# Softmax rows of an attention layer split into fp16 halves and transposed by DMA instead of TensorE

## The chip, the cores and the metric

The kernel runs on one core of a Trainium2 chip. The number is device time in microseconds for one launch. Before the change it is 2286.52 us, the median of three runs (2285.9 to 2289.88). All times of single instructions are from one profiled execution.

## What is computed

The input x is 128 examples of 128 tokens by 384 channels, and adj holds one 128x128 matrix per example. Two layers follow each other, both with a residual. Layer A is attention with 12 heads of 32 channels and a full bias of 2·adj; layer B has three causal "experts" of 128 channels, mixed by a gate.

```python
# layer A (x here is the layernormed input)
q = (x @ Wq.T), k = (x @ Wk.T), v = (x @ Wv.T + bv)      # 12 heads of 32
scores = einsum('bqhd,bkhd->bhqk', q, k) * scale + 2 * adj[:, None]
p = softmax(scores)                                      # rows that are all zero give 0
out = einsum('bhqk,bkhd->bqhd', p, v) @ Wo.T + bo
# layer B (x here is the layernormed sum)
q, k = x @ Wqk + bqk; expert 0's q goes through a 3-tap convolution over tokens
expert 1 takes 4 global keys more (masked by the causal mask, as columns past 128)
y_e = causal_softmax(q_e k_e^T / sqrt(128)) @ (x @ Wv[e] + bv[e])
out = (y * gate_weights) @ Wp + bp                       # top 2 of 3 experts
```

## The kernel before

The 128 examples are worked in 32 groups of four. Matmuls on projections are done in three fp16 passes (hi·hi, hi·lo, lo·hi), where each fp32 operand has been split into a rounded fp16 part and an fp16 remainder. ScalarE writes the rounded part (called hi), VectorE the remainder (lo). Scores, softmax and the mix p·v of layer A work in fp32, the scores on stacked fp16 parts in one matmul.

Nothing is scheduled at run time. Five tables of words give the order of the steps on TensorE (`pe`), ScalarE (`act`), VectorE (`dve`), GpSimd (`pool`) and the SyncE queue (`sp`). Each engine goes through its list strictly in order and waits on semaphores. `FIRST_STEPS` and `LAST_STEPS` are the ramps; `ORDER_OF_STEPS` is one turn, repeated 30 times. A word such as `A.mix.2` is step mix of layer A for example 2 of the group; `A.score.2.1` is the second third (four heads) of example 2. In one turn the engines work on three groups: the layer-A steps that `ahead` names (hT, qk, stack) on the newest, the rest of layer A on the one before it, layer B on the one before that.

The steps of layer A for one example b, with the lines of the profile:

- *hT*: GpSimd writes the normed rows (L1082), ScalarE (L699) and VectorE (L948) split them, and SyncE issues a DMA that transposes both fp16 parts through the crossbar (L495, tile h1T). *qk*, *v*: projections (L534). *stack*: 24 SBUF-to-SBUF DMAs in each group lay the parts of q and k out for the scores (L509, tiles Qs and Ks); the first score of a group waits for all 24.
- *score*: four heads a step on TensorE (L603); VectorE adds the bias, takes the row minimum of the negated score and writes raw_score (L978). *smax* (L984) reads raw_score once more for the maximum. ScalarE takes the exponential out of raw_score into S[b % 2] with the row sum (L738). *norm*: VectorE makes the row factor, GpSimd multiplies S by it in three pieces (L1125).
- *turn*: TensorE transposes S, four heads a step (L616), and ScalarE moves the result from PSUM to PT (L752). *mix*: 12 fp32 matmuls with 32 columns of v (L628), which land in four column strips of the array. *proj*: VectorE adds the residual xres (L1021), which GpSimd has made of xin and bo_row (L1111). *ln2* prepares layer B.

PSUM has a ring of five banks for A and three for B; a step on TensorE waits until the step five (three) places before it on its layer's list has been evacuated.

## Time and profile before

| | |
|---|---|
| runs | 2286.52 us (2285.9 to 2289.88) |
| profiled execution | 2291.18 us, of which the span from first to last instruction is 2289.4 us |
| busy share of the span | PE 95%, DVE 81%, ACT 65%, POOL 51% |
| granted TensorE clock | 0.991 of full speed |
| DMA engines | 29.9% of the 16 engines' span in the main queue |

PE is TensorE's matmul unit, DVE is VectorE, ACT is ScalarE, POOL is GpSimd, SP the SyncE queue. A row's "busy" is the time covered by its instructions; since instructions of one engine overlap at their ends, the distance from start to start is the cost of a step in a row of steps, and the mean duration is somewhat more than that. A DMA has two times: what its issue takes on the SP queue, and the time until it has landed.

### The profile page before, as it was taken

How to read it: one execution, taken by the hardware profiler on the slowest of the kernel's cores; microseconds unless marked ns; L12 is line 12 of the kernel's file. 1: busy time of each engine (PE TensorE's matmuls, PEld its weight loads, DVE VectorE, ACT ScalarE, POOL GpSimd, SP SyncE). 2: the span in 40 equal slices, each digit the busy share in tenths (PEclk: the TensorE clock that was granted, in tenths of full speed). 3: DMA queues.
4: the chain of work that ended last, by engine and by line, in shares of the span. 5: the costliest groups of instructions: out<-in, count | busy, mean ns of one | idle time of the engine just before them, and what ended most of it. 6: DMA issues, size and time to landing. Idle time of an engine off the chain costs nothing.

```text
span 2289.4 us, 51173 instructions
## 1 busy us (share of the span) xinstructions
PE 2172.9 (95%) x16557; PEld 1385.8 (61%) x16557; DVE 1855.0 (81%) x7182; ACT 1492.9 (65%) x5330; POOL 1159.8 (51%) x1553
## 2 busy tenths in 40 slices
PE   4699999999999999999999999999999999999998
PEld 2366666666666666666656666656666656666655
DVE  5788887888888788887778887888887888877884
ACT  2676666676666676666666665766666766666763
POOL 2645554455554455554445554455555455554452
PEclk9899999999999999999999999999999999999999
DMA  6312334322333322323313333223333223333210
GB/s 186 70 38 70 88 75 89 73 48 71 89 75 89 72 48 72 88 75 88 72 43 77 84 79 88 60 50 83 78 85 89 59 50 83 79 85 89 44 32 28
DMA packets 244665, 168.36 MB, mean 74 GB/s; under 512 B 119216, under 2 KB 243760, under 8 KB 244400
## 3 DMA queue, kind: packets, MB, share of 16 engines
q1 hardware_dynamic: 242208, 163.80, 29.9%
q8 instruction: 134, 2.20, 0.4%
q10 hardware_dynamic: 2192, 1.29, 0.2%
q14 instruction: 131, 1.07, 0.2%
HBM read 39.18 MB, written 25.17 MB: 28 GB/s over the span
## 4 chain that ended last, share of the span: by engine, by line
PE 78%; DVE 9%; DMA 5%; ACT 3%; SPq 2%; issue 2%; POOL 1%; POOLq 0%; DVEq 0%
PE A_bank L534 30%; PE B_bank L534 24%; PE A_bank L616 6%; DMA h1T<-h_parts 4%; PE B_bank L610 4%; PE A_bank L628 4%; PE B_bank L635 4%; PE A_bank L603 3%; DVE smax L984 3%; DVE h_parts L948 2%; PE B_bank L620 2%; PE B_bank L580 2%; DVE raw_score L978 2%; ACT h_parts L699 1%; POOL h L1082 1%
## 5 line engine op out<-in xcount | busy, mean ns | idle before, releaser
L738 ACT ACTIVATE S<-raw_score,smin 128x128 f32<-128x128 f32 x1536 | 594.9, 393 | 94.6 <-DVE smin L978 94.6
L1125 POOL TENSOR_TENSOR S<-S,rowf 128x512 f32<-128x512 f32 x384 | 415.7, 1110 | 398.3 <-DVE rowf L1003 398.3
L978 DVE CUSTOM_DVE_ANT_0 raw_score<-A_bank,adj,s_unit 128x128 f32<-128x128 f32 x1536 | 433.5, 345 | 18.6 <-PE A_bank L603 15.9
L1130 POOL TENSOR_TENSOR S<-S,row2f 128x384 f32<-128x384 f32 x128 | 105.8, 826 | 499.6 <-DVE row2f L1011 496.8
L738 ACT ACTIVATION_READ_ACCUMULATOR S<-raw_score,smin 128x1 f32 x1536 | 294.7, 192 | 0.0
L534 PE MATMUL A_bank<-h1T,wq_hi 128*128 128x512 f16 x576 | 177.0, 390 | 76.4 <-DMA h1T<-h_parts 76.3
L616 PE MATMUL A_bank<-ident,S 128*128 128x128 f32 x1536 | 218.2, 275 | 5.5 <-POOL S L1125 5.5
L984 DVE TENSOR_REDUCE smax<-raw_score 128x12 f32<-128x1536 f32 x128 | 223.0, 1743 | 0.0
L752 ACT ACTIVATE PT<-A_bank 128x512 f32<-128x512 f32 x384 | 210.3, 591 | 6.7 <-PE A_bank L616 6.0
L534 PE MATMUL A_bank<-wv_hi,h1T 128*128 128x384 f16 x768 | 199.3, 328 | 5.9 <-DVE wv_lo L771 5.0
L616 PEld LDWEIGHTS A_bank<-ident,S 128*128 128x128 f32 x1536 | 178.2, 142 | 31.6 <-issue 11.7
L703 ACT ACTIVATE b_hT_hi<-B_bank 128x512 f16<-128x512 f32 x96 | 53.2, 587 | 190.4 <-PE B_bank L580 190.4
L534 PE MATMUL A_bank<-h1T,wk_hi 128*128 128x512 f16 x576 | 171.3, 379 | 0.7 <-DVE smin L978 0.7
L752 ACT ACTIVATE PT<-B_bank 128x384 f32<-128x384 f32 x128 | 62.8, 491 | 160.0 <-PE B_bank L620 159.8
L1082 POOL TENSOR_SCALAR h<-xin,stat 128x384 f32<-128x384 f32 x128 | 89.2, 699 | 129.0 <-DVE h_parts L948 128.7
L745 ACT ACTIVATE S<-S,s2min 128x128 f32<-128x128 f32 x384 | 149.0, 395 | 3.8 <-DVE s2min L988 3.8
L603 PE MATMUL A_bank<-Ks,Qs 96*128 96x128 f16 x1536 | 133.8, 219 | 3.5 <-DMA Ks<-k_hi 2.3
L534 PEld LDWEIGHTS A_bank<-h1T,wq_hi 128*128 128x128 f16 x576 | 53.7, 99 | 136.9 <-issue 74.3
L988 DVE CUSTOM_DVE_ANT_0 S<-B_bank,later 128x128 f32<-128x128 f32 x384 | 90.9, 286 | 55.6 <-PE B_bank L610 55.3
L603 PEld LDWEIGHTS A_bank<-Ks,Qs 96*128 96x128 f16 x1536 | 110.6, 98 | 36.3 <-issue 3.2
L534 PE MATMUL B_bank<-wv2g_hi,b_hT_hi 128*128 128x416 f16 x384 | 130.2, 339 | 0.0
L534 PE MATMUL B_bank<-wv2g_hi,b_hT_lo 128*128 128x416 f16 x384 | 130.1, 339 | 0.0
(183 smaller groups left out, 5975.6 us busy)
## 6 DMA issues: line engine op xcount, KB each, us to landing
xin<-in_x SPq DMA_DIRECT2D x32, 768.0 KB, 4.9
Qs<-q_hi SPq DMA_DIRECT2D x256, 96.0 KB, 2.2
out<-x1res SPq DMA_DIRECT2D x128, 192.0 KB, 2.1
Ks<-k_hi SPq DMA_DIRECT2D x252, 96.0 KB, 3.2
Qs<-q_lo SPq DMA_DIRECT2D x128, 96.0 KB, 2.2
Ks<-k_lo SPq DMA_DIRECT2D x126, 96.0 KB, 2.9
adj<-in_adj SPq DMA_DIRECT2D x32, 256.0 KB, 5.7
h1T<-h_parts SPq DMA_TRANSPOSE x128, 2.9
```

The costliest lines, as they stand in the source:

```text
L534: mm = nc.tensor.matmul(dst, left(c)[a], right(c)[b], start=(c == 0 and n == 0), stop=(c == KC - 1 and n == 2))
L603: mm = nc.tensor.matmul(dst[:, tok(j)], Qs[:, c * HPC + j, tok(b)], Ks[:, c * HPC + j, tok(b)], start=True, stop=True)
L610: mm = nc.tensor.matmul(dst[:, tok(e)], q2[:, e, tok(b)], k2[:, e, tok(b)], start=True, stop=True)
L616: mm = nc.tensor.transpose(dst[:, tok(j)], S[b % 2][:, c * HPC + j, :], ident[:])
L738: ins = nc.scalar.activation(S[b % 2][:, h, :], raw_score[:, h, :], ACT.Exp, bias=smin[b % 2][:, h:h + 1], scale=-1.0, accum_out=ssum[b % ...
L745: ins = nc.scalar.activation(S2[b % 2][:, e, :], S2[b % 2][:, e, :], ACT.Exp, bias=s2min[b % 2][:, e:e + 1], scale=-1.0, accum_out=s2sum[b ...
L752: nc.scalar.activation(dst, src[:, 0:dst.shape[1]], ACT.Copy).then_inc(evacuated[stage, "act"], 1)
L978: ins = nc.vector.tensor_tensor_reduce(raw_score[:, h, :], src[:, j * T:(j + 1) * T], adj2[:, b, :], s_unit[:], 3.0e38, ALU.add, ALU.min, ...
L984: nc.vector.tensor_reduce(smax[b % 2][:], raw_score[:], AXX, ALU.max).then_inc(maxed, 1)
L1082: nc.gpsimd.tensor_scalar(h1[:, b % 2, :], xin[g % 2][:, b, :], stat[g % 2][:, 0, b:b + 1], stat[g % 2][:, 1, b:b + 1], ALU.add, ALU.mult) ...
L1125: nc.gpsimd.tensor_tensor(S[b % 2][:, hs, :], S[b % 2][:, hs, :], rowf[b % 2][:, hs].unsqueeze(2).broadcast_to([P, HPC, T]), ALU.mult).the ...
L1130: nc.gpsimd.tensor_tensor(S2[b % 2][:], S2[b % 2][:], row2f[b % 2][:].unsqueeze(2).broadcast_to([P, NE, T]), ALU.mult).then_inc(normed2, 1)
```

## The change

The softmax rows of layer A no longer go through TensorE to be transposed. After the row factor has been applied (it now holds 2^14 more, so that fp16 has range), ScalarE rounds each third of S to fp16 and GpSimd subtracts to get the remainder. SyncE issues one crossbar transpose per third, with both parts, into PT. The values v are split in the same way: VectorE writes V, ScalarE the fp16 part, GpSimd the remainder (step vl). The mix takes 36 fp16 matmuls in place of 12 fp32 ones and the factor 2^-14 is taken out when its result is split.

Besides: the exponential is taken in place, with S[b % 2] in the place of raw_score, so it now waits for smax (`maxed`); the scores of example b wait until the remainder of example b-2 has been taken (`p_lo`). The residual is added into xin in place, so the load of x for the group after next waits for the group's last proj and goes to the end of the SP list. h1_parts is a ring of two. The row guard in norm is a chain of four small instructions, as before. The first gate step is one instruction shorter. Scores of layer B wait for the turn of two examples before. All order tables are new.

```diff
+P_SCALE = 2.0 ** 14
 def ahead(step):
-    return step[0] == "A" and step[1] in ("hT", "qk", "stack", "h1")
+    return step[0] == "A" and step[1] in ("ln1", "h1", "hT", "qk", "stack")
...
-        xres = sb("xres", [P, GB, C])
-        h1_parts = sb("h1_parts", [P, GB, 2, C], F16)
+        h1_parts = sb("h1_parts", [P, 2, 2, C], F16)
-        V = sb("V", [P, GB, C])
+        V = sb("V", [P, 2, C])
+        V_parts = sb("V_parts", [P, GB, 2, C], F16)
-        raw_score = sb("raw_score", [P, NH, T])
-        PT = [sb(f"PT{k}", [P, HPC * T]) for k in range(KC)]
+        P_parts = sb("P_parts", [P, KC, 2, HPC * T], F16)
+        PT = [sb(f"PT{k}", [P, KC, 2 * HPC, T], F16) for k in range(2)]
@@ SyncE @@
-                if (stage, kind) == ("A", "res") and g + 2 < NG:
-                    sp.wait_ge(xres_ready, count(g, GB, GB))
-                    sp.wait_ge(h1_ready, count(g, GB, GB))
+                if (stage, kind) == ("A", "load") and g + 2 < NG:
+                    wait_evacuated(sp, ("A", "proj", GB - 1, 0), g)
                     sp.dma_start(xin[g % 2][:], dram_group(x, g + 2)).then_inc(x_loaded[g % 2], 16)
+                if (stage, kind) == ("A", "turn"):
+                    sp.wait_ge(p_lo, count(g, GB * KC, b * KC + third + 1))
+                    if third == 0 and b >= 2:
+                        wait_products(sp, ("A", "mix", b - 2, 0), g)
+                    elif third == 0 and not g == 0:
+                        wait_products(sp, ("A", "mix", b + 2, 0), before(g))
+                    sp.dma_start_transpose(PT[b % 2][:, third, :, :],
+                                           P_parts[:, third, :, :].rearrange("p n k -> p (n k)"))\
+                        .then_inc(p_turned[third], 16)
@@ TensorE @@
-                elif kind == "turn" and A:
-                    pe.wait_ge(normed, count(g, GB * KC, b * KC + c + 1))
-                    for j in range(HPC):
-                        mm = nc.tensor.transpose(dst[:, tok(j)], S[b % 2][:, c * HPC + j, :], ident[:])
                 elif kind == "mix" and A:
-                    wait_evacuated(pe, ("A", "v", b, 0), g)
+                    pe.wait_ge(v_lo, count(g, GB, b + 1))
                     for k in range(KC):
-                        wait_evacuated(pe, ("A", "turn", b, k), g)
-                        for j in range(HPC):
-                            h = k * HPC + j
-                            mm = nc.tensor.matmul(dst[j * HD:(j + 1) * HD, tok(k)], V[:, b, h * HD:(h + 1) * HD],
-                                                  PT[k][:, tok(j)],
-                                                  start=True, stop=True)
+                        pe.wait_ge(p_turned[k], count(g, 16 * GB, 16 * (b + 1)))
+                        for n, (v_part, p_part) in enumerate([(0, 0), (1, 0), (0, 1)]):
+                            for j in range(HPC):
+                                h = k * HPC + j
+                                mm = nc.tensor.matmul(dst[j * HD:(j + 1) * HD, tok(k)],
+                                                      V_parts[:, b, v_part, h * HD:(h + 1) * HD],
+                                                      PT[b % 2][:, k, p_part * HPC + j, :],
+                                                      start=(n == 0), stop=(n == 2))
@@ ScalarE @@
+                if kind == "v":
+                    wait_evacuated(act, step, g)
+                    if not g == 0:
+                        wait_products(act, ("A", "mix", b, 0), before(g))
+                    nc.scalar.activation(V_parts[:, b, 0, :], V[:, b % 2, :], ACT.Copy).then_inc(v_hi, 1)
+                elif kind == "turn" and A:
+                    act.wait_ge(normed, count(g, GB * KC, b * KC + c + 1))
+                    if not (g == 0 and b == 0):
+                        act.wait_ge(p_turned[c], count(g, 16 * GB, 16 * b))
+                    nc.scalar.activation(P_parts[:, c, 0, :],
+                                         S[b % 2][:, c * HPC:(c + 1) * HPC, :].rearrange("p j k -> p (j k)"),
+                                         ACT.Copy).then_inc(p_hi, 1)
                 elif kind == "score" and A:
                     wait_evacuated(act, step, g)
+                    act.wait_ge(maxed, count(g, GB, b + 1))
-                        ins = nc.scalar.activation(S[b % 2][:, h, :], raw_score[:, h, :], ACT.Exp,
+                        ins = nc.scalar.activation(S[b % 2][:, h, :], S[b % 2][:, h, :], ACT.Exp,
@@ VectorE @@
                 elif kind == "score" and A:
-                    if not (g == 0 and b == 0):
-                        dve.wait_ge(exped, count(g, GB * KC, (b - 1) * KC + c + 1))
-                        dve.wait_ge(maxed, count(g, GB, b))
+                    if b >= 2 or not g == 0:
+                        dve.wait_ge(p_lo, count(g, GB * KC, (b - 2) * KC + c + 1))
                 elif kind == "score":
+                    if b >= 2:
+                        wait_products(dve, ("B", "turn", b - 2, 0), g)
+                    elif not g == 0:
+                        wait_products(dve, ("B", "turn", b + 2, 0), before(g))
@@ GpSimd @@
+                elif kind == "vl":
+                    pool.wait_ge(v_hi, count(g, GB, b + 1))
+                    nc.gpsimd.tensor_tensor(V_parts[:, b, 1, :], V[:, b % 2, :], V_parts[:, b, 0, :],
+                                            ALU.subtract).then_inc(v_lo, 1)
+                elif kind == "turn":
+                    pool.wait_ge(p_hi, count(g, GB * KC, b * KC + c + 1))
+                    nc.gpsimd.tensor_tensor(P_parts[:, c, 1, :],
+                                            S[b % 2][:, c * HPC:(c + 1) * HPC, :].rearrange("p j k -> p (j k)"),
+                                            P_parts[:, c, 0, :],
+                                            ALU.subtract).then_inc(p_lo, 1)
-                    nc.gpsimd.tensor_tensor(xres[:, b, :], xin[g % 2][:, b, :], bo_row[:], ALU.add).then_inc(xres_ready, 1)
+                    pool.wait_ge(h1_ready, count(g, GB, b + 1))
+                    nc.gpsimd.tensor_tensor(xin[g % 2][:, b, :], xin[g % 2][:, b, :], bo_row[:],
+                                            ALU.add).then_inc(xres_ready, 1)
```

One row of the new table, as a specimen (SyncE's turn; the row of before is `A.hT.0 A.hT.1 A.hT.2 A.hT.3 A.stack.0 A.res A.adj A.stack.1 B.proj.0 ...`):

```diff
+        A.hT.0 A.turn.0.0 A.hT.1 A.turn.0.1 A.turn.0.2 A.hT.2 A.hT.3 A.turn.1.0 A.turn.1.1 A.turn.1.2 A.adj
+        A.turn.2.0 A.turn.2.1 A.turn.2.2 A.stack.0 A.turn.3.0 A.turn.3.1 A.turn.3.2 A.stack.1 B.proj.0 B.proj.1
+        B.proj.2 B.proj.3 A.load
```

The order on three engines, in the middle of a steady turn. First SyncE's queue over one turn, before, with its DMAs in the order of their issue:

```order
L495 DMA_TRANSPOSE h1T<-h_parts 128x6x128 x4
L509 DMA Qs<-q_hi 32x3x512 x8
L509 DMA Qs<-q_lo 32x3x512 x4
L488 DMA xin<-in_x 128x4x384
L514 DMA adj<-in_adj 128x4x128
L509 DMA Ks<-k_hi 32x3x512 x4
L509 DMA Ks<-k_lo 32x3x512 x4
L509 DMA Ks<-k_hi 32x3x512 x4
L517 DMA out<-x1res 128x384 x4
```

And now, from the last two transposes of h1T on (ahead of them stand two of h1T and the three of example 0, taking turns):

```order
L501 DMA_TRANSPOSE h1T<-h_parts 128x6x128 x2
L510 DMA_TRANSPOSE PT<-P_parts 128x8x128 x3
L530 DMA adj<-in_adj 128x4x128
L510 DMA_TRANSPOSE PT<-P_parts 128x8x128 x3
L525 DMA Qs<-q_hi 32x3x512 x8
L525 DMA Qs<-q_lo 32x3x512 x4
L510 DMA_TRANSPOSE PT<-P_parts 128x8x128 x3
L525 DMA Ks<-k_hi 32x3x512 x4
L525 DMA Ks<-k_lo 32x3x512 x4
L525 DMA Ks<-k_hi 32x3x512 x4
L533 DMA out<-x1res 128x384 x4
L494 DMA xin<-in_x 128x4x384
```

Twelve transposes of eight blocks each have come in, three of them between the stacking of q and that of k, and the load of x has moved to the end.

Then GpSimd from the norm of example 1 to that of example 3, before (S<-S,rowf is the norm of layer A, S<-S,row2f that of layer B, h<-xin the normed rows of the next group):

```order
L1125 TENSOR_TENSOR S<-S,rowf 128x512 x3
L1082 TENSOR_SCALAR h<-xin,stat 128x384 x4
L1125 TENSOR_TENSOR S<-S,rowf 128x512 x3
L1130 TENSOR_TENSOR S<-S,row2f 128x384 x2
L1120 TENSOR_TENSOR x1res<-x,bp_row 128x384
L1125 TENSOR_TENSOR S<-S,rowf 128x512 x3
```

And the same stretch now (P_parts<-S,P_parts is the remainder of a third of the softmax rows, V_parts<-V,V_parts that of v):

```order
L1167 TENSOR_TENSOR S<-S,rowf 128x512 x3
L1137 TENSOR_TENSOR V_parts<-V,V_parts 128x384
L1141 TENSOR_TENSOR P_parts<-S,P_parts 128x512 x3
L1167 TENSOR_TENSOR S<-S,rowf 128x512 x3
L1141 TENSOR_TENSOR P_parts<-S,P_parts 128x512 x2
L1162 TENSOR_TENSOR x1res<-x,bp_row 128x384
L1141 TENSOR_TENSOR P_parts<-S,P_parts 128x512
L1152 TENSOR_TENSOR xin<-xin,bo_row 128x384
L1137 TENSOR_TENSOR V_parts<-V,V_parts 128x384
L1152 TENSOR_TENSOR xin<-xin,bo_row 128x384
L1167 TENSOR_TENSOR S<-S,rowf 128x512 x3
```

Between two norms there are now three subtractions of 128x512 that were not there, and the normed rows of the next group have moved ahead of this piece.

Last, TensorE around the mix of example 0, before:

```order
L534 MATMUL B_bank<-b_hT_hi,wk_lo 128x512
L628 MATMUL A_bank<-PT,V 32x128 x12
L616 MATMUL A_bank<-ident,S 128x128 x8
L534 MATMUL B_bank<-b_hT_hi,wk_hi 128x512
L534 MATMUL B_bank<-b_hT_lo,wk_hi 128x512
```

And now:

```order
L618 MATMUL A_bank<-Ks,Qs 128x128 x8
L639 MATMUL A_bank<-PT,V_parts 32x128 x36
L618 MATMUL A_bank<-Ks,Qs 128x128 x4
L550 MATMUL A_bank<-h1T,wq_hi 128x512 x2
L550 MATMUL A_bank<-h1T,wq_lo 128x512
```

The transposes are gone, a mix has 36 short matmuls, and the first mix stands between the scores of example 3, where before it came ahead of them.

## Rows read from the trace of the kernel before

**Rows 1.** The page's busy times: engine, busy us, share, instructions.

```profile
PE 2172.9 (95%) x16557; PEld 1385.8 (61%) x16557; DVE 1855.0 (81%) x7182; ACT 1492.9 (65%) x5330; POOL 1159.8 (51%) x1553
```

**Rows 2.** The page's chain that ended last, by engine.

```profile
PE 78%; DVE 9%; DMA 5%; ACT 3%; SPq 2%; issue 2%; POOL 1%; POOLq 0%; DVEq 0%
```

**Rows 3.** Timeline of the SP queue: start, duration, instruction; a turn's first transposes.

```profile
139.89 6.46 SPq L495 DMA_TRANSPOSE h1T<-h_parts  x4
...
2138.67 6.47 SPq L495 DMA_TRANSPOSE h1T<-h_parts  x4
```

**Rows 4.** Windows, one turn: length, busy per engine, clock, DMA share, GB/s.

```profile
1033.46:1102.14 68.68, 67.01 (x518) 42.87 (x517) 56.97 (x224) 45.89 (x167) 35.70 (x48) 1.00 0.32 74
```

**Rows 5.** Timeline of PE: start, duration to the last end, instruction, idle before.

```profile
1027.64 0.83 PE L603 MATMUL A_bank<-Ks,Qs 96*128 96x128 f16 x12
1028.31 0.38 PE L534 MATMUL B_bank<-b_hT_hi,wk_hi 128*128 128x512 f16 x1
...
1030.35 0.86 PE L628 MATMUL A_bank<-PT,V 128*32 128x128 f32 x24
1031.14 1.09 PE L616 MATMUL A_bank<-ident,S 128*128 128x128 f32 x8
...
1041.73 0.59 PE L534 MATMUL A_bank<-h1T,wq_hi 128*128 128x512 f16 x2 [1.67 <-DMA h1T<-h_parts]
...
1047.71 1.04 PE L616 MATMUL A_bank<-ident,S 128*128 128x128 f32 x8
1048.58 0.83 PE L610 MATMUL B_bank<-k,q 128*128 128x128 f32 x6
```

**Rows 6.** Lines: out<-in, count, busy us, mean ns, idle before.

```profile
L1092 POOL TENSOR_TENSOR wq_lo<-x,wq_hi 128x1152 f16<-128x1152 f32 x1 | 2.4, 2367 | 0.1
...
L1111 POOL TENSOR_TENSOR xres<-xin,bo_row 128x384 f32<-128x384 f32 x128 | 127.8, 1009 | 0.0
...
L1082 POOL TENSOR_SCALAR h<-xin,stat 128x384 f32<-128x384 f32 x128 | 89.2, 699 | 129.0 <-DVE h_parts L948 128.7
...
L699 ACT ACTIVATE h_parts<-h 128x384 f16<-128x384 f32 x128 | 66.6, 520 | 89.5 <-POOL h L1082 89.4
...
L738 ACT ACTIVATE S<-raw_score,smin 128x128 f32<-128x128 f32 x1536 | 594.9, 393 | 94.6 <-DVE smin L978 94.6
...
L984 DVE TENSOR_REDUCE smax<-raw_score 128x12 f32<-128x1536 f32 x128 | 223.0, 1743 | 0.0
...
L948 DVE SCALAR_TENSOR_TENSOR h_parts<-h,h_parts 128x384 f16<-128x384 f32 x128 | 70.3, 570 | 56.9 <-ACT h_parts L699 56.9
...
L828 DVE BATCH_NORM_STATS2 bn<-xin 128x6 f32<-128x384 f32 x128 | 61.7, 545 | 5.3 <-DMA xin<-in_x 5.3
```

**Rows 7.** Timeline of DVE: one norm, two evacuations of v, 12 heads of scores.

```profile
1017.96 0.17 DVE L995 TENSOR_SCALAR live<-smin 128x12 f32<-128x12 f32 x1
...
1018.53 1.14 DVE L967 SCALAR_TENSOR_TENSOR V<-A_bank,v_unit,bv_row 128x384 f32<-128x384 f32 x2
1019.59 0.34 DVE L978 CUSTOM_DVE_ANT_0 raw_score<-A_bank,adj,s_unit 128x128 f32<-128x128 f32 x1
...
1022.84 0.65 DVE L967 SCALAR_TENSOR_TENSOR V<-B_bank,v_unit,bvg_row 128x416 f32<-128x416 f32 x1
```

**Rows 8.** Line L1125, the norm on POOL: duration in ns min/median/max.

```profile
L1125 POOL TENSOR_TENSOR S<-S,rowf x384: 1033/1039/1480, 64.5 to 2228.0; 128x512 f32<-128x512 f32 x192
```

**Rows 9.** Line L1043, half of the convolution on DVE: the same.

```profile
L1043 DVE SCALAR_TENSOR_TENSOR q<-q2raw,conv_neg,q x32: 748/1406/1407, 133.5 to 2258.0; 128x508 f32<-128x508 f32 x32
```

**Rows 10.** Line L495, the crossbar transposes: duration on SP, then time to landing.

```profile
L495 SPq DMA_TRANSPOSE h1T<-h_parts x128: 1210/1286/2862, 20.8 to 2143.8; - x128
...
DMA to landing us min/median/max: 2.8/2.9/6.1
```

**Rows 11.** Timeline of the SP queue: start and duration of eight stacking DMAs.

```profile
1056.78 5.13 SPq L509 DMA_DIRECT2D Qs<-q_hi  x8
```

**Rows 12.** The page's DMA issues: count, KB each, median us to landing.

```profile
Ks<-k_hi SPq DMA_DIRECT2D x252, 96.0 KB, 3.2
```

More of the change, by code:

```diff
@@ L123 @@
-        A.adj@0 A.stack.0@1 A.stack.1@1
+        A.hT.0@0 A.hT.1@0 A.hT.2@0 A.hT.3@0 A.stack.0@0 A.stack.1@0 A.hT.0@1 A.hT.1@1 A.hT.2@1 A.hT.3@1
+        A.turn.0.0@0 A.turn.0.1@0 A.turn.0.2@0 A.turn.1.0@0 A.turn.1.1@0 A.turn.1.2@0 A.stack.0@1 A.turn.2.0@0
+        A.turn.2.1@0 A.turn.2.2@0 A.adj@0 A.turn.3.0@0 A.turn.3.1@0 A.turn.3.2@0 A.stack.1@1 A.load@0
     """,
```

278 lines of the change are left out of this document (141 added, 137 removed).

## The prediction

> **What bounds the kernel now.** I read the busy times first, then the chain, then one turn. TensorE is busy 95% of the span and VectorE 81%, while ScalarE (65%) and GpSimd (51%) have room [rows 1]; 78% of the chain that ended last is TensorE's [rows 2]. The reader should not stop at the 95%: whether it is a bound or a mean is decided inside one turn. From the first crossbar transpose of a turn to that of the next, 29 turns take 2138.67 - 139.89 = 1998.8 us, 68.9 each [rows 3]; what is left of the 2289.4, some 290 us, is the two ramps. One such turn has TensorE busy for 67.0 of 68.7 us, VectorE 57.0, ScalarE 45.9, GpSimd 35.7, at the full granted clock [rows 4]. The one gap of TensorE is 1.67 us, the wait for h1T [rows 5]. So a turn is TensorE's work plus 1.7 us, and a microsecond off TensorE is worth one only until another engine's list, or a loop through several, takes as long.
>
> **TensorE's ledger.** Eight transposes take 1048.58 - 1047.71 = 0.87 us, so a step of four 0.435, and the twelve steps that go 5.2 us a turn. The fp32 mix takes 1031.14 - 1030.35 = 0.79 us; four go, 3.2 us [rows 5]. What comes is not in the trace: 36 fp16 matmuls with 32 columns of weights. From below: the scores, also fp16 and 128 long, are 0.67/12 = 0.056 us apart [rows 5]; if the four column strips always ran at once, 36 x 0.056/4 = 0.50. From above: one after another, 36 x 0.056 = 2.0. The nearest row is the old mix itself, in the same strips, with 24 records in 0.79, 0.033 each; I take 36 x 0.033 = 1.19, or 4.8 a turn (2.0 to 8.1). TensorE's work becomes 67.0 - 5.2 - 3.2 + 4.8 = 63.4 us, and 60.6 or 66.7 at the ends.
>
> **GpSimd's ledger.** Twelve remainders of 128x512 and four of 128x384 come in. The nearest row is the subtraction that made a weight's remainder, fp32 less fp16, 2367 ns for 1152 columns [rows 6]: 1.05 and 0.79 us, in all 12.6 + 3.2. From above the residual's rate, 1009 ns for 384 [rows 6], gives 1.35 and 1.01, in all 20.2. The residual in place costs what it did. So 35.7 + 15.8 = 51.5 us, below the turn, but GpSimd also has a loop. It ends a turn with the last normed rows of layer B, and its next big piece, norm of example 0, needs, on other engines: the B transposition and its two evacuations (0.44 + 0.52 + 0.57, by the A ones), the maximum 1.74, two more evacuations 1.1, four statistics 2.2, two thirds of a score 2.2 and the row factor 0.57: together 9.4 [rows 5 to 7]. Meanwhile it can do a residual, a remainder and two normed rows, 1.0 + 0.8 + 1.4. With some 1 us of waiting for each of three later row factors the loop is 51.5 + 9.4 - 3.2 + 3 = 60.7.
>
> **The loop through VectorE and SyncE.** The exponential now waits for the maximum, the scores of example b for the remainders of b-2, and behind VectorE's wait stand its evacuations, so PSUM's rings. VectorE's list from the first score of a turn to the last maximum holds four scores of 3.25, four maxima of 1.74, eight evacuations of v at 0.53 to 0.65, eight of about 0.57, statistics 2.2, three row factors of 0.57 and the convolution at about 2.2: 35.4 us [rows 6, 7, 9]. Then follow, with nothing beside them: twelve exponentials at 0.39 = 4.7, the row factor 0.6, GpSimd's norm 3 x 1.04, two norms of layer B 1.6 and the scaling of adj 0.9 (both by their width), and the last remainders 3.2 [rows 6, 8]; the issue of the last transpose, which I scale by its blocks, 1.29 x 8/6 = 1.7 [rows 10]; and behind it on SyncE's queue the twelve DMAs that stack k, 0.64 each = 7.7, the last of which lands 2.6 after its issue [rows 11, 12]. Only then can the next turn's first score start: 35.4 + 4.7 + 0.6 + 8.8 + 1.7 + 7.7 + 2.6 = 61.5. Before, no transpose stood ahead of these DMAs. SyncE's own issues, 12 x 1.7 + 4 x 1.3 + 24 x 0.64 and some 4 of loads and stores, are 45 us and fit.
>
> **The small edits.** ScalarE gives up 12 evacuations and does 12 roundings of the same width and four of 0.52 [rows 6]: 2 us on an engine with over 20 to spare. The load of x waits for the last proj; its consumer, the statistics, comes some 9 us into the next turn, so I count nothing, and up to 2 us a turn if it lands late. The exponential in place costs VectorE nothing by itself. In the first ramp h1_parts makes the third split wait for a landing, 2.9 us once [rows 10]; the last ramp saves one group's 3.6 us of TensorE. I leave the ramps as they are, 5 us either way.
>
> **What two rows say about GpSimd and VectorE together.** The norm on GpSimd takes 1039 ns in the median and up to 1480 [rows 8]; half of the convolution takes 748 ns at best and 1406 as a rule [rows 9], in a stretch where GpSimd is at a norm. One of them holds the other up by 0.4 to 0.7 us. GpSimd goes from 36 to 52 us a turn, so row factors, splits and gate pieces on VectorE will meet it more often. I put one and a half such delays of 0.66 on the loop, 1.0 us. The Trainium skill (SBUF — State Buffer, Who interferes with whom) says why: a VectorE instruction with two SBUF inputs and a GpSimd instruction that reads SBUF exclude each other for a whole instruction. The trace agrees, with 1406 against 748; by the rule taken strictly, some thirty small VectorE instructions a turn could each be held up, which is the rival on GpSimd below.
>
> **The sum.** 63.4 of TensorE, 1.7 of waits as today, 1.0 of delays: 66.1 us a turn, with loops of 60.7 and 61.5 below it that I cannot price closer than a few us. 68.9 - 66.1 = 2.8, times 29 turns = 82 us. The profiled execution, 2291.2 of which 2289.4 are the span, would become 2209; it lies 4.7 above the median of the runs, 2286.5, so I predict 2204.
>
> **Rivals.**
>
> 1. *More is gained*: the mix runs all strips at once, 0.50, and the delays stay off the path. 60.6 + 1.7 = 62.3 a turn, 6.6 x 29 = 192, so 2095. For it: four strips already overlap. Against: the two loops are as long as this. 0.10.
> 2. *The transposes land late*: they share the DMA engines with 24 stacking DMAs a turn, and the longest landing is 6.1 against 2.9 [rows 10]. The last mix of a turn waits for the last transpose. With half of that, 1.6 us, a turn is 67.7: 2251. Against it: the median landing with four in a row is 2.9. 0.15.
> 3. *Nothing is left*: waits eat what TensorE gives, 68.9 again, 2286. 0.04.
> 4. *GpSimd becomes the bound, and it is slower*: if norms (mean 1.11 now, 415.7/384 busy) and remainders all ran at the worst ratio seen, 1480/1039, that is 12 x 0.4 + 12 x 0.45 + 4 x 0.33 = 11 us on a loop of 60.7: 71.7 a turn, 2286 + 2.8 x 29 = 2367. It decides from 8.2 us more in that loop, when GpSimd's own work passes 59.7. For it: two engines that were rarely busy together will be. Against: most of VectorE's large pieces read PSUM and one SBUF tile. 0.18.
> 5. *The crossbar is slow*: the longest landing, 6.1 for six blocks, as a rule of 1.02 a block, times 24 + 96 blocks, is 122 us a turn, 2286 + 53 x 29 = 3820. Against it: four transposes are issued in 6.5 us and land 2.9 after their issue [rows 3, 10]. 0.02. The Trainium skill (VectorE: DVE Perf Modes, The three transpose paths) gives 1309 ns for a 128x128 block by DMA and 390 on TensorE; by that, 120 blocks one after another would be an estimated 157 us a turn. The trace does not bear it out: 24 blocks are through in under 10 us.
>
> **The numbers.** The forecast has 0.51, with its own range of 2150 to 2242 (64.2 to 67.4 a turn). The range of 8 in 10 is 2095 to 2310: it takes in rivals 1 to 3 and the near part of 4. Faster by over 0.2% (4.6 us, about what a measurement here can tell from nothing) is the forecast with rivals 1 and 2, 0.76; within it 0.04; slower 0.20.
>
> **What would show it.** Right: a turn near 66 us between first transposes; a mix of about 1.2 us; remainders of about 1.05 us; transposes of P issued in about 1.7 us; TensorE busy near 63 of 66 at full clock, with its longest wait at the first score of a turn, for the stacked k. Wrong: remainders above 1.4 us and GpSimd over 60 us a turn (rival 4); mixes that wait on landings of 4 us and more (2); a granted clock under 1.00 in the middle of a turn, which would say that the new waits are long enough to lower it, and which I give no term.

## The result, and the profile after

The changed kernel takes 2333.1 us (median of 4 runs, 2332.0 to 2333.2) beside 2288.2 for the kernel before: 1.020 times as long, 95% interval 1.018 to 1.021. I had predicted 2204, in a range of 2095 to 2310.

The page after has the same parts as before; first the busy times, then the chain, beside [rows 1, 2].

```profile
PE 2044.0 (88%) x16557; PEld 1229.2 (53%) x16557; DVE 2092.0 (90%) x7150; ACT 1576.0 (68%) x5458; POOL 1739.9 (75%) x2065
...
DVE 55%; PE 20%; POOL 12%; issue 10%; SPq 1%; DMA 1%; ACT 1%; DVEq 0%; POOLq 0%; ACTq 0%
```

TensorE's busy time fell by 129 us (my ledger had 3.6 a turn, 115 in 32). VectorE, to whose list the prediction added nothing but its 1.0 us a turn of delays, gained 237 us, and the chain is now its chain. One turn, from one load of adj to the next (windows view; columns as in [rows 4]):

```profile
1071.16:1141.00 69.84, 63.54 (x517) 38.66 (x516) 63.49 (x215) 48.56 (x171) 52.82 (x64) 0.98 0.56 117
```

And SyncE's timeline, the first transposes of h1 in the second and in the last turn, beside [rows 3]:

```profile
140.32 1.27 SPq L501 DMA_TRANSPOSE h1T<-h_parts  x1
...
2172.13 1.27 SPq L501 DMA_TRANSPOSE h1T<-h_parts  x1
```

A turn takes (2172.13 - 140.32)/29 = 70.06 us against 68.92: 33 of the 42 us by which the span grew. The other 9 are the two ramps. TensorE and VectorE are both busy for 63.5 of 69.8 us, so neither is a bound by itself: a loop through both is.

Where did VectorE's 237 us go? The groups of instructions by line, beside [rows 6, 9]:

```profile
L1014 DVE TENSOR_REDUCE smax<-S 128x12 f32<-128x1536 f32 x128 | 223.1, 1743 | 0.1
...
L974 DVE SCALAR_TENSOR_TENSOR h_parts<-h,h_parts 128x384 f16<-128x384 f32 x128 | 144.0, 1143 | 15.4 <-ACT h_parts L725 15.2
...
L921 DVE SCALAR_TENSOR_TENSOR q2raw<-V,wg_row 128x128 f32<-128x128 f32 x96 | 77.2, 855 | 0.1
L1047 DVE TENSOR_TENSOR row2f<-r2inv,g_w 128x3 f32<-128x3 f32 x128 | 59.4, 464 | 4.4
L1079 DVE SCALAR_TENSOR_TENSOR q<-q2raw,conv_neg,q 128x508 f32<-128x508 f32 x32 | 48.0, 1499 | 1.1
L1076 DVE SCALAR_TENSOR_TENSOR q<-q2raw,conv_neg,q 128x508 f32<-128x508 f32 x32 | 44.4, 1389 | 0.0
```

The maximum takes what it took, 1743 ns. The split of h1 doubled, 570 to 1143; each gate product takes 855 (287 before); the first half of the convolution 1389 (741 before, the second went from 1384 to 1499). What these have in common shows best where one source line makes both kinds (the view of line L974: ns min/median/max):

```profile
L974 DVE SCALAR_TENSOR_TENSOR h_parts<-h,h_parts x128: 558/957/1427, 10.8 to 2180.6; 128x384 f16<-128x384 f32 x128
L974 DVE SCALAR_TENSOR_TENSOR b_hT_lo<-B_bank,b_hT_hi x96: 678/681/692, 126.4 to 2291.2; 128x512 f16<-128x512 f32 x96
```

It is the same operation, on rows of 384 and 512. With both inputs in SBUF it takes 558 to 1427 ns; with one in PSUM 678 to 692, always. GpSimd was busy for 35.7 us of a turn before [rows 4]; now it is for 52.8. The timelines of GpSimd and of VectorE at one gate:

```profile
1003.97 1.16 POOL L1141 TENSOR_TENSOR P_parts<-S,P_parts 128x512 f16<-128x512 f32 x1
1005.08 1.05 POOL L1152 TENSOR_TENSOR xin<-xin,bo_row 128x384 f32<-128x384 f32 x1
1006.10 0.96 POOL L1137 TENSOR_TENSOR V_parts<-V,V_parts 128x384 f16<-128x384 f32 x1
```

```profile
1005.20 1.09 DVE L921 SCALAR_TENSOR_TENSOR q2raw<-V,wg_row 128x128 f32<-128x128 f32 x1
...
1006.21 1.00 DVE L921 SCALAR_TENSOR_TENSOR q2raw<-V,wg_row 128x128 f32<-128x128 f32 x1
```

The two products end at 1006.29 and 1007.21, each some 0.15 us after the GpSimd instruction beside it (1006.13, 1007.06). That is what waiting for it looks like, rather than running slowly. What the two wait for is a residual sum and the remainder of v, not a remainder of P; only the first product of a turn meets one of those. Layer B's transposes wait for this gate, and TensorE for them (timeline of PE):

```profile
1002.45 0.83 PE L625 MATMUL B_bank<-k,q 128*128 128x128 f32 x6
...
1014.89 0.52 PE L630 MATMUL B_bank<-ident,S 128*128 128x128 f32 x3 [1.87 <-POOL S L1172]
...
1015.96 1.48 PE L625 MATMUL B_bank<-k,q 128*128 128x128 f32 x6
```

After the wait the same six matmuls take 1.48 in place of 0.83: for a part of this stretch the granted clock was at its lower level (1.2 in place of 2.4 GHz). The windows view has 0.64 as its mean:

```profile
1014.90:1019.30 4.40, 4.40 (x55) 4.06 (x56) 2.86 (x15) 2.53 (x9) 4.30 (x5) 0.64 0.42 83
```

TensorE's waits in the whole run (us in total, times, longest) name VectorE's evacuations and layer B's normed rows, and hardly the stacked k, for which I had looked:

```profile
PE B_bank L550 <- DVE V L998: 75.9, 30, 2.6
PE B_bank L630 <- POOL S L1172: 63.7, 33, 10.3
...
PE A_bank L618 <- DMA Ks<-k_hi: 4.5, 3, 4.1
```

The crossbar (duration on SyncE's queue in ns, then us to landing), beside [rows 10]:

```profile
L510 SPq DMA_TRANSPOSE PT<-P_parts x384: 1231/1248/2478, 74.4 to 2277.9; - x192
...
DMA to landing us min/median/max: 3.0/3.2/5.5
```

### The profile page after: what moved, and what is told of

It reads as the page before. It is cut to its first block, busy times and chain, and to the rows that moved or that the text cites. A ratio compares the mean times of both kernels' runs of the same rounds, so it can differ in the third digit from the quotient of the medians.

```text
span 2331.3 us, 53112 instructions
## 1 busy us (share of the span) xinstructions
PE 2044.0 (88%) x16557; PEld 1229.2 (53%) x16557; DVE 2092.0 (90%) x7150; ACT 1576.0 (68%) x5458; POOL 1739.9 (75%) x2065
## 4 chain that ended last, share of the span: by engine, by line
DVE 55%; PE 20%; POOL 12%; issue 10%; SPq 1%; DMA 1%; ACT 1%; DVEq 0%; POOLq 0%; ACTq 0%
DVE S L1008 12%; PE B_bank L550 8%; PE A_bank L550 7%; DVE smax L1014 6%; DVE h_parts L974 5%; DVE V L998 5%; POOL h L1185 3%; POOL rstd L1182 3%; DVE S L1022 3%; DVE b_hT_lo L974 2%; DVE q2raw L921 2%; DVE bn L855 2%; DVE q_lo L980 2%; DVE row2f L1047 1%; PE B_bank L630 1%
## 5 line engine op out<-in xcount | busy, mean ns | idle before, releaser
L765 ACT ACTIVATE S<-S,smin 128x128 f32<-128x128 f32 x1536 | 593.3, 388 | 47.9 <-DVE smax L1014 47.8
L1141 POOL TENSOR_TENSOR P_parts<-S,P_parts 128x512 f16<-128x512 f32 x384 | 476.3, 1256 | 9.3 <-ACT P_parts L706 7.2
L1008 DVE CUSTOM_DVE_ANT_0 S<-A_bank,adj,s_unit 128x128 f32<-128x128 f32 x1536 | 431.9, 343 | 15.0 <-PE A_bank L618 14.6
L765 ACT ACTIVATION_READ_ACCUMULATOR S<-S,smin 128x1 f32 x1536 | 288.0, 188 | 0.0
L706 ACT ACTIVATE P_parts<-S 128x512 f16<-128x512 f32 x384 | 229.0, 619 | 43.0 <-POOL S L1167 42.8
L1014 DVE TENSOR_REDUCE smax<-S 128x12 f32<-128x1536 f32 x128 | 223.1, 1743 | 0.1
L550 PE MATMUL B_bank<-b_hT_hi,wk_hi 128*128 128x512 f16 x288 | 117.1, 407 | 75.9 <-DVE V L998 75.9
L974 DVE SCALAR_TENSOR_TENSOR h_parts<-h,h_parts 128x384 f16<-128x384 f32 x128 | 144.0, 1143 | 15.4 <-ACT h_parts L725 15.2
L1137 POOL TENSOR_TENSOR V_parts<-V,V_parts 128x384 f16<-128x384 f32 x128 | 128.2, 1002 | 28.9 <-ACT V_parts L700 28.9
L550 PE MATMUL B_bank<-wp_hi,yT_hi 128*128 128x384 f16 x384 | 125.0, 325 | 11.4 <-DVE yT_lo L990 10.4
L1152 POOL TENSOR_TENSOR xin<-xin,bo_row 128x384 f32<-128x384 f32 x128 | 131.1, 1025 | 0.8 <-DMA bo_row<-in_a_bo 0.8
```

The costliest lines, as they stand in the source:

```text
L550: mm = nc.tensor.matmul(dst, left(c)[a], right(c)[b], start=(c == 0 and n == 0), stop=(c == KC - 1 and n == 2))
L706: nc.scalar.activation(P_parts[:, c, 0, :], S[b % 2][:, c * HPC:(c + 1) * HPC, :].rearrange("p j k -> p (j k)"), ACT.Copy).then_inc(p_hi, 1)
L765: ins = nc.scalar.activation(S[b % 2][:, h, :], S[b % 2][:, h, :], ACT.Exp, bias=smin[b % 2][:, h:h + 1], scale=-1.0, accum_out=ssum[b % 2 ...
L974: nc.vector.scalar_tensor_tensor(out=lo, in0=rows_in, scalar=H_SCALE, in1=hi, op0=ALU.mult, op1=ALU.subtract)\
L1008: ins = nc.vector.tensor_tensor_reduce(S[b % 2][:, h, :], src[:, j * T:(j + 1) * T], adj2[:, b, :], s_unit[:], 3.0e38, ALU.add, ALU.min, s ...
L1014: nc.vector.tensor_reduce(smax[b % 2][:], S[b % 2][:], AXX, ALU.max).then_inc(maxed, 1)
```

## The experiments

Theory 1: VectorE is held up by GpSimd's reads (1a), or GpSimd's list is itself too long for its loop (1b). Theory 2: the transposes or the new order. Theory 3: the clock. "Turn" is between first transposes of h1, as above. All ratios are to the kernel before, with their 95% interval.

| kernel | us | ratio | turn | DVE busy | POOL busy |
|---|---|---|---|---|---|
| before | 2288 | | 68.92 | 1855 | 1160 |
| after | 2333 | 1.018 to 1.021 | 70.06 | 2092 | 1740 |
| p_lo_off | 2223 | 0.970 to 0.973 | 66.73 | 1936 | 1271 |
| p_lo_memset | 2231 | 0.973 to 0.976 | 66.83 | 1970 | 1643 |
| fills_126 | 2228 | 0.971 to 0.975 | 66.77 | 1963 | 1696 |
| fills_184 | 2431 | 1.060 to 1.064 | 73.27 | 2012 | 1893 |
| half_read | 2313 | 1.010 to 1.013 | 69.45 | 2022 | 1717 |
| one_input | 2268 | 0.989 to 0.994 | 67.95 | 2041 | 1687 |
| fine | 2417 | 1.055 to 1.058 | 72.88 | 2047 | 1900 |
| gate_old | 2383 | 1.040 to 1.043 | 71.75 | 2100 | 1737 |
| two_pass | 2216 | 0.967 to 0.970 | 66.49 | 1932 | 1271 |
| res_early | 2281 | 0.996 to 0.998 | 68.34 | 2061 | 1734 |
| two_pass_res | 2207 | 0.963 to 0.966 | 66.15 | 1932 | 1260 |

**The remainders, with and without their reads.** p_lo_off drops GpSimd's remainders (SyncE waits for the high part), p_lo_memset puts fills in their place:

```diff
-nc.gpsimd.tensor_tensor(P_parts[:, c, 1, :], S[...], P_parts[:, c, 0, :], ALU.subtract).then_inc(p_lo, 1)
+nc.gpsimd.memset(P_parts[:, c, 1, :], 0.0).then_inc(filled, 1)      # p_lo_memset
+pool.wait_ge(filled, ...)
+nc.gpsimd.memset(P_parts[:, c, 1, :], 0.0).then_inc(p_lo, 1)
```

> The kernel after, without GpSimd's twelve remainders of the softmax rows in a turn: the low part of P is zeroed once and stays zero, so the third pass of the mix adds nothing; the transposes, the 36 matmuls and the order of the rest are those of the kernel after. Theory 1 (the time went to GpSimd's new work and the VectorE instructions that wait for it to leave SBUF): GpSimd falls by some 15 us a turn, VectorE's busy time from 2092 to some 1900 us, the split of h1 from 1143 to under 800 ns, and the time to 2130 to 2210 us. Theory 2 (the transposes, SyncE's queue or the new order hold the turn up, whatever GpSimd does): the time stays at 2290 us or more. Theory 3 (TensorE's granted clock, which falls after waits, is the cause): 2250 to 2300, since nothing here works on the clock directly.

> The kernel after, with each of GpSimd's twelve remainders of the softmax rows replaced by two fills with zeros of the same 128x512 fp16 tile, some 1.1 us together: GpSimd's list stays about as long, but the fills read nothing (the low part of P is left out). Theory 1a (VectorE is held up by GpSimd's reads): the split of h1 falls from 1143 to under 850 ns, the gate's three products from 855 to under 600, VectorE's busy time to under 1980 us, and the time to 2180 to 2270 us. Theory 1b (GpSimd's list itself is too long for its loop with the transposition of layer B): VectorE's rows may fall, but the time stays at 2310 to 2340.

2223 and 2231 us, far under the 2290 of theory 2, though p_lo_off lies above the 2130 to 2210 that I had given theory 1 (the split of h1 at 896, not under 800). GpSimd's 372 us of difference between the two cost 8; the other 102 are the reads and some 0.15 us of list for each remainder. In p_lo_memset the gate's products were to fall under 600 ns. They did not:

```profile
L922 DVE SCALAR_TENSOR_TENSOR q2raw<-V,wg_row 128x128 f32<-128x128 f32 x96 | 68.1, 763 | 0.1
```

Two of the three still meet the residual sums and the remainder of v, which read as before, and yet the time is down by 102. So what holds the gate up is not by itself what the 102 us are. To hold the list still, fills_126 has three fills (512, 320 and 256 columns) and fills_184 four (512, 512, 512, 64):

> p_lo_memset (2231 us) with three fills in place of two, of 512, 320 and 256 columns, some 1.26 us together as the remainder took in the kernel after (the low part of P is left out). GpSimd's list is then as long as in the kernel after and still reads nothing more. Theory 1a (VectorE's held-up instructions set the turn): 2230 to 2250 us, since 12 x 0.2 us on GpSimd hide. Theory 1b (what the reads cost is the 0.2 us by which the remainders themselves are held up on GpSimd): 2280 to 2330 us.

> p_lo_memset with fills of 512, 512, 512 and 64 columns, some 1.8 us together, as long as the four pieces of the remainder in the kernel fine (2417 us); the low part of P is left out. This gives the slope: GpSimd's list gets 12 x 0.75 = 9 us longer a turn than in p_lo_memset. If the list is the bound of fine and is near it in the kernel after: 2350 to 2430 us. If VectorE's waits are what made fine slow: under 2290.

fills_126 has GpSimd's list as long as after (three fills of 524, 364 and 311 ns and two gaps of 58 between them are 1.32 us, a remainder 1.26) and takes 2228, 105 us less. So the reads of the remainders cost these 105 us, and 1a holds for them as a whole. Its groups by line, and the split of h1 by its own view (min/median/max):

```profile
L922 DVE SCALAR_TENSOR_TENSOR q2raw<-V,wg_row 128x128 f32<-128x128 f32 x96 | 22.0, 282 | 0.1
...
L1077 DVE SCALAR_TENSOR_TENSOR q<-q2raw,conv_neg,q 128x508 f32<-128x508 f32 x32 | 23.7, 742 | 0.0
...
L975 DVE SCALAR_TENSOR_TENSOR h_parts<-h,h_parts x128: 543/559/1392, 11.3 to 2081.0; 128x384 f16<-128x384 f32 x128
```

The gate's products are back at 282 ns (they now stand beside fills), the convolution at 742. Of the four splits of h1 in a turn two are free, beside fills, and two still meet GpSimd's norm: the median went from 957 to 559, the mean from 1143 to 851. One turn of it, in the windows view:

```profile
1026.00:1092.40 66.40, 62.11 (x516) 37.26 (x516) 60.31 (x222) 47.80 (x169) 51.99 (x89) 1.00 0.59 122
```

fills_184 shows where 1b begins: its fills take 1.90 us with their gaps, so 12 x 0.58 = 7.0 us more of list raise the turn by 6.5. In fills_126 the loop through GpSimd was already within about half a us of deciding.

half_read keeps the remainders of examples 0 and 2 and fills for 1 and 3:

> Between the kernel after (2333 us, twelve remainders a turn that read) and fills_126 (2228 us, fills that read nothing and take as long): examples 0 and 2 of a group keep their remainders, 1 and 3 get the fills (their low part of P is left out). If the cost goes by the number of reads: 2270 to 2295 us. If it is made by the reads that meet the gate and the convolution late in the turn (examples 2 and 3): within 25 us of one of the two ends.

2313, 20 us below after: half of the reads cost 85 of the 105 us, so it does not go by their number. The gate's products and the split of h1 were as in the kernel after (853 and 1142 ns), the convolution free (742):

```profile
L975 DVE SCALAR_TENSOR_TENSOR h_parts<-h,h_parts 128x384 f16<-128x384 f32 x128 | 143.9, 1142 | 15.6 <-ACT h_parts L726 15.5
```

What a read costs depends on what it meets. Beside p_lo_memset, which has the gate at 763 and lost its 102 us, the largest row that differs is this split, 1142 against 846. TensorE's wait for the evacuation of v, which stands behind the splits on VectorE's list, fits: 75.9 us in half_read as in the kernel after, 38.8 in p_lo_memset. So the splits are the likely carrier of a good part of the 105 us, but no run frees them alone, and res_early, below, gets 52 us back with the split at 1133.

**The same in the kernel before.** Sixteen remainders of 128x416, or thirty-two fills of 128x448, behind the normed rows, on constant tiles:

```diff
 ALU.mult).then_inc(normed, 1)
+for _ in range(2 if n == KC - 1 else 1):          # before_read
+    nc.gpsimd.tensor_tensor(spare[:], bvg_row[:], WQ_hi[...], ALU.subtract).then_inc(filled, 1)
```

> The kernel before, with sixteen remainders of 128x416 a turn added on GpSimd behind the normed rows, on constant tiles; nobody waits for them. Theory 1a: VectorE's instructions with two SBUF inputs grow as they did in the kernel after, the split of h1 from 570 to 850 ns or more, VectorE's busy time from 1862 by 80 to 220 us; TensorE hides most of it, so the time is 2290 to 2360. If GpSimd's reads don't hold VectorE up: VectorE's rows stay within 5% of before's.

> The kernel before, with thirty-two fills of a constant tile of 128x448 a turn added on GpSimd at the same places, which read nothing and take about as long as the sixteen remainders of the kernel beside it. Theory 1a: VectorE's rows stay as before, the split of h1 at 570 to 620 ns, and the time within 15 us of 2288 or what GpSimd's longer list alone costs. If any GpSimd work slows VectorE: the split of h1 grows to 850 ns as in the kernel beside it.

2590 (ratio 1.130 to 1.134) and 2554 (1.113 to 1.117). I expected TensorE to hide them; it doesn't. In the order of before, GpSimd's longer list, with what the fills hold up, costs 266 us, the reads 37 more. Here the gate's products, before_read first:

```profile
L898 DVE TENSOR_TENSOR q2raw<-g_hid,wg_row 128x128 f32<-128x128 f32 x96 | 54.7, 621 | 1.1
```

```profile
L898 DVE TENSOR_TENSOR q2raw<-g_hid,wg_row 128x128 f32<-128x128 f32 x96 | 23.1, 296 | 1.1
```

621 with reads, 296 with fills (287 in the kernel before). The split of h1 did not grow (574 and 566), so that part of my expectation was wrong: it is not held up in that order. And the order of after carries nearly as long a list of fills (fills_126, 15.8 us a turn) at 2228; with 16.2 us the order of before takes 2554. A tensor_scalar, the first step of the old gate (217 ns in the kernel before), is held up by both, before_read first:

```profile
L896 DVE TENSOR_SCALAR g_hid<-V 128x128 f32<-128x128 f32 x32 | 20.6, 644 | 0.0
```

```profile
L896 DVE TENSOR_SCALAR g_hid<-V 128x128 f32<-128x128 f32 x32 | 17.3, 541 | 0.0
```

**Clock and crossbar.** fill adds 24 transposes of the identity ahead of TensorE's wait for layer B's first normed rows; two_pass leaves the low part of P out of transposes and mix.

```diff
+if b == 0:                                        # fill
+    for _ in range(24): nc.tensor.transpose(dst[:, tok(0)], ident[:], ident[:])
 pe.wait_ge(normed2, count(g, GB, b + 1))
-enumerate([(0, 0), (1, 0), (0, 1)])               # two_pass
+enumerate([(0, 0), (1, 0)])
-sp.dma_start_transpose(PT[b % 2][:, third, :, :], P_parts[:, third, :, :]...)
+sp.dma_start_transpose(PT[b % 2][:, third, 0:HPC, :], P_parts[:, third, 0, :])
```

> The kernel after, with 24 transposes of the identity (about 0.11 us each, 2.6 us) that TensorE does ahead of its wait for the first normed rows of layer B in each group, in the bank that it is about to write; nobody reads them. Theory 3 (the lowered clock behind that wait costs time by itself): the granted clock rises from 0.974 to 0.985 or more, and the time falls by 20 to 60 us. Theory 1 (VectorE's list sets the turn and the clock follows from the waits): the clock may rise but the time stays within 10 us of 2333.

> The kernel after without the low part of P altogether: no remainder on GpSimd, transposes of four blocks in place of eight, and a mix of two passes (24 matmuls in place of 36). Beside p_lo_off, 2223 us, it takes away half of the crossbar's work for P and a third of the mix. Theory 2 in its weaker form (crossbar, DMA or SyncE still hold something up): under 2190 us. Theory 1 (they are hidden, VectorE and what waits for it set the turn): 2205 to 2228 us, with the mix near 0.4 us in place of 0.6.

fill: 2350 us (1.026 to 1.029), 17 more than after, and the clock rose only from 0.974 to 0.976. It did not keep the clock up, so it doesn't price it, and theory 3 is left open; in fills_126 the clock was 0.991 without any such help. two_pass is 7 us faster than p_lo_off: half of the crossbar's work for P and the third pass are hidden but for that. Theory 2, as it was put, falls; what the order alone can do, res_early shows below.

**Finer pieces, one input, the gate as it was.** fine cuts the remainder into four of 128x128 (fine_norm the normed rows too); one_input takes one input from nine VectorE instructions a turn (four splits, three products, two halves of the convolution; "ten" in its expectation is a slip); gate_old undoes one edit.

```diff
-nc.gpsimd.tensor_tensor(P_parts[:, c, 1, :], S[...], P_parts[:, c, 0, :], ALU.subtract)        # fine
+for j in range(HPC): nc.gpsimd.tensor_tensor(P_parts[:, c, 1, tok(j)], S[...], P_parts[:, c, 0, tok(j)], ALU.subtract)
-nc.vector.scalar_tensor_tensor(out=lo, in0=rows_in, scalar=H_SCALE, in1=hi, ...)               # one_input
+nc.vector.tensor_scalar(lo, rows_in, 0.0, 0.0, ALU.mult, ALU.mult)
-v.scalar_tensor_tensor(out=g_prod[:, e], in0=V2[...], scalar=0.0, in1=wg2_row[...], ...)       # gate_old
+link(v.tensor_scalar(g_hid[:], V2[:, :, C:VG], 0.0, None, ALU.max))
+v.tensor_tensor(g_prod[:, e], g_hid[:], wg2_row[...], ALU.mult)
```

> The kernel after, with each of GpSimd's 128x512 remainders of the softmax rows cut into four of 128x128, so the same elements are read in pieces a quarter as long. Theory 1a (a VectorE instruction with two SBUF inputs waits for a whole GpSimd instruction to end): its waits shrink with the piece, the split of h1 from 1143 to 900 ns or less, the conv's first half from 1389 to under 1100, the gate's products from 855 to under 600, and the time to 2250 to 2310 us although GpSimd's remainders get longer in all. If the two engines only share bandwidth, by bytes: VectorE's rows stay within 10% and the time is 2330 or more.

> The kernel fine, with the normed rows cut too: instead of three products of 128x512 with a broadcast factor, twelve of 128x128 with one factor for each partition, so all of GpSimd's softmax work goes in pieces of 128x128. Theory 1a: VectorE's rows fall below those of fine (the split of h1 under 800 ns, the factor row2f from 464 to under 300), and the time to 2210 to 2280 us, unless GpSimd's twelve pieces take over 4.5 us an example, when its list gives it back. Otherwise: as fine or slower.

> The kernel after with GpSimd's work unchanged, and one SBUF input fewer in ten of VectorE's instructions a turn: the split of h1 writes zeros from h1 alone (its low part is left out), the gate's three products leave out the weight row, and the two halves of the convolution scale q in place (its outer taps are left out). Theory 1a (these instructions wait for GpSimd): they come near what they take alone, 0.3 to 0.6 us each, VectorE's busy time falls by some 200 us, and the time to 2200 to 2270 us. Theory 1b (GpSimd's list): GpSimd's remainders lose their delays only in part, and the time stays above 2300.

> The kernel after with the gate's first step as it was in the kernel before: one instruction that takes the maximum with zero, and three products, in place of three merged ones. If each of these VectorE instructions waits for half a GpSimd instruction or so: four waits in place of three, 0.3 to 0.9 us more a turn, 2333 to 2360 us. If the merged form is what is slow (the products went from 287 to 855 ns): under 2320.

fine: 2417, not the 2250 to 2310 that I had given. VectorE's busy time fell by 45 us (split of h1 893 ns, convolution 742, but the gate's products 825 in the mean). Four pieces keep GpSimd busy for 1.70 us (652.7/384) against 1.24, so its list is as long as in fills_184 (1900 and 1893 us), which takes 2431 with no reads in the pieces' place. The 825 hides two things (view of line L921):

```profile
L921 DVE SCALAR_TENSOR_TENSOR q2raw<-V,wg_row x96: 277/509/4678, 164.6 to 2388.1; 128x128 f32<-128x128 f32 x96
```

In the median a product takes 509 ns, where the kernel after has 1002: the wait does shrink with the piece. But nine of the 96 take 4.5 to 4.7 us. The one that starts at 526.93 ends at 531.59, after GpSimd has gone through a series of eight instructions up to 531.45. A wait is thus not always for one instruction. fine_norm: 2524 (1.102 to 1.105), not 2210 to 2280, with normed pieces of 408 ns; its split of h1, 1323 in the mean where I had said under 800, is 676 in the median and 3607 at most. With GpSimd's list this long neither run tells what shorter waits would be worth in time.

one_input: 2268, a gain of 65 and inside my 2200 to 2270, but VectorE's busy time fell by 51 us, not by some 200, for the instructions still wait (groups by line):

```profile
L972 DVE TENSOR_SCALAR h_parts<-h 128x384 f16<-128x384 f32 x128 | 118.9, 947 | 15.4 <-ACT h_parts L725 15.3
...
L921 DVE TENSOR_SCALAR q2raw<-V 128x128 f32<-128x128 f32 x96 | 67.6, 756 | 0.1
```

A tensor_scalar with one SBUF input is held up too, so this run does not give the price of a second input. The Trainium skill (SBUF — State Buffer, Who interferes with whom) says that a tensor_scalar in a mode that uses both port pairs contends with GpSimd, and that two SBUF inputs contend with its reads and not with its writes. The traces agree: beside fills the tensor_scalar takes 541 ns for 217, while the products right behind it take 296 for 287. That these tensor_scalars run in such a mode no trace here shows.

gate_old: 2383, 49 us slower than after and above my 2360. One more VectorE instruction ahead of the gate and products of 1004 ns make the turn 1.7 us longer. So the merged gate, which I did not price, is worth 49 us in this kernel.

**Versions.** two_pass_hT moves the split of h1 from VectorE to GpSimd, two_pass_hT_row also the product for row2f:

```diff
+nc.gpsimd.tensor_tensor(h1_parts[:, b % 2, 1, :], h1[:, b % 2, :], h1_parts[:, b % 2, 0, :], ALU.subtract)
```

> The kernel two_pass (2216 us; it leaves the low part of P out), with the split of h1's low part moved from VectorE to GpSimd, which has room there: four subtractions of 128x384 a turn, with the factor 64 taken into the rstd of layer A's norm. VectorE loses 4 x 0.9 us a turn and cannot be held up there any more; GpSimd gets 4 x 1.0 us. If VectorE's list is still the longest part of the loop: 2120 to 2190 us. If TensorE and the waits between engines are: 2195 to 2220. If GpSimd's longer list or the later landing of h1T counts: above 2220.

> The kernel beside it, with the small product of layer B's row factor (128x3, four a turn, 0.33 us each with its wait) moved to GpSimd too, just ahead of the normed rows that use it. Off VectorE and off one hand-over between engines in the loop through layer B's transposes: 5 to 40 us faster than the kernel beside it; nothing, if these stand off the path.

2278 (0.994 to 0.998) and 2324 (1.014 to 1.017), both far slower than two_pass, though VectorE's busy time fell to 1875 and 1840. GpSimd goes through its list in order, and among its waits in two_pass_hT stands the split that I had put there:

```profile
POOL h_parts L1185 <- ACT h_parts L725: 133.9, 63, 12.4
```

134 us of waiting, with the rest of its list behind it: the likely reason, which no run tries by itself. Last, the place of the reads: res_early moves GpSimd's residual sums in its order, with all the work and nothing left out.

```diff
-B.res.0 A.vl.0 A.ln1 ... A.turn.0.2 A.res.0 A.h1.3 ... A.turn.2.2 A.res.1 A.vl.2 A.res.2 A.norm.3 ... A.ln2.0 A.res.3 A.ln2.1
+B.res.0 A.vl.0 A.res.0 A.res.1 A.res.2 A.res.3 A.ln1 ... A.turn.0.2 A.h1.3 ... A.turn.2.2 A.vl.2 A.norm.3 ... A.ln2.0 A.ln2.1
```

> The kernel after with all its work, and one change of order: GpSimd's four residual sums of layer A (128x384, 1.0 us each) stand ahead of layer A's statistics, where GpSimd waited 4.5 us a turn for VectorE, in place of the gate's neighbourhood and the end of the turn. Theory 1 (a VectorE instruction waits for the GpSimd instruction that is reading, and the gate lies on the path): the gate's products fall from 855 ns, the loop through GpSimd gets some 3 us shorter, and the time falls by 30 to 90 us, to 2245 to 2300. If the place of the reads doesn't matter, since their number is the same: within 15 us of 2333.

> As res_early, with the residual sum of layer B that stood between the remainders of example 2 moved to GpSimd's wait ahead of the second normed rows. Theory 1: another 0 to 30 us below res_early; slower than it by up to 20 us, if that wait was needed by the normed rows behind it.

> The same change of order as in res_early made in two_pass (2216 us, the low part of P left out), whose gate products are at 304 ns already. Theory 1: little is left to gain, 2190 to 2220 us. If the gain of the order comes from GpSimd's shorter list and not from the gate: as many us less as between the kernel after and res_early.

res_early: 2281, 52 us below after and 7 (0.3%) below before; with res_early_b the only version of full work that is not slower than before. Its gate:

```profile
L921 DVE SCALAR_TENSOR_TENSOR q2raw<-V,wg_row 128x128 f32<-128x128 f32 x96 | 48.6, 558 | 0.1
```

558 ns for 855 is 0.9 us a turn, of 1.7 that it gained. But the sums now also fill a wait of GpSimd's, for the statistics of layer A, which fell from 145.2 us in the run to 32.5. Which of the two the gain came from isn't shown. res_early_b brings the products to 320 ns and the time stays, 2282 (0.996 to 0.999): by then the gate no longer decides. two_pass_res gains 9 us, to 2207; with the gate free and GpSimd's list short from the start, it can't tell the two apart either.

## Why the prediction was wrong

- **TensorE's ledger** held to 1.3 us. I had 63.4 us a turn; fills_126, in a turn at full clock, shows 62.1, with the mix at 0.62 in place of 1.19. The mix alone would make it 61.1, so a miss of 1.0 the other way helped. That the kernel after shows 63.5 is luck: it has matmuls at the lower clock in it.
- **What two rows say about GpSimd and VectorE together** is the step that failed. I read the right mechanism from two rows and put 1.5 delays of 0.66 on the loop, 1.0 us a turn. VectorE's busy time says (2092.0 - 1963.2)/32 = 4.0 us, and the turn 70.06 - 66.77 = 3.3. I counted the delays that I had seen, not the instructions that could meet one: by the excess over fills_126 it is three gate products at 0.57, two halves of the convolution at 0.65 and 0.73, four splits of h1 at 0.29 and four row factors row2f at 0.27, 5.3 us in all; small ones that are longer in fills_126 give 1.2 back. Not all of the 5.3 is the remainders' direct doing: two of the gate's products wait for other GpSimd instructions, and it was the shift in the list that freed them. With 1.0 replaced by 3.3 my sum is 68.4, a little under before still, so this step makes 2.3 of the 4.0 us by which the turn passed my 66.1.
- **The missing bound** makes the other 1.7: I took TensorE and the 1.7 us of waits of before for the turn, and never added the delays to VectorE's own list. It was 57.0 us a turn and became 63.5 (60.3 in fills_126, so half of the growth is not from the remainders' reads), with gate, layer B's normed rows, TensorE's tail, ln2 and the transposition of layer B behind one another; that chain, not TensorE, ends the turn. It is VectorE's chain without those reads too: 54% of the span in p_lo_memset. Free of them the turn is 66.8, 1.7 more than 63.4 + 1.7, and with 1.7 taken as this rest the parts add up to 70.1 by construction. The waits themselves are more than that. In the turn of fills_126 shown above TensorE is idle for 66.40 - 62.11 = 4.3 us, mostly for VectorE's evacuation of v and for GpSimd's norm of layer B (its waits, beside the 75.9 and 63.7 of the kernel after):

```profile
PE B_bank L551 <- DVE V L999: 52.5, 30, 1.8
PE B_bank L631 <- POOL S L1175: 43.2, 33, 6.8
```

- **GpSimd's ledger.** 52.8 us a turn against 51.5; a remainder has 1162 ns in the median, 1256 in the mean, against 1.05. Its loop, which I put at 60.7, stands at about 66 (fills_184). Five us short, and without effect only because the turn without reads is about as long. Rival 4 named the right pair of engines and the right sign, but its mechanism, GpSimd's list, does not decide here: fills_126 is as long and 105 us faster.
- **The loop through VectorE and SyncE** did not decide: TensorE waited 4.5 us in the whole run for the stacked k. It is not far off: in fills_126 the chain is 3% SyncE's queue and 3% DMA. Transposes were issued in 1.25 us and landed in 3.2; rivals 2 and 5 are out.
- **Small edits at nothing:** the gate is worth 49 us in the changed kernel, in its favour.
- **The clock:** 0.974. I said that it would show waits long enough to lower it, and gave it no term. The same 16557 matmuls are busy for 2044.0 us here and 2010.3 in fills_126, so by estimate up to 34 of the 105 us are matmuls at the lower clock, behind those waits; no run parts the clock from the waits, so what it costs stays open. **The ramps** cost 9 us, against 5 either way.
